# The last stage's normalisation beside the attention before it, and two jobs for GpSimd

## The chip, the cores and the metric

One core of a Trainium2 chip runs the whole program in one launch. The metric is the device time of one execution in microseconds (us). The engines are TensorE (PE, matmuls and transposes), VectorE (DVE), ScalarE (ACT), GpSimd (POOL) and SyncE (SP, which only issues transfers). Each engine works through its own list of instructions in order and waits on semaphores; a wait holds back everything behind it on that engine.

## The reference, cut to what matters

x is 128 sequences of 64 rows of 128 numbers. Four layers follow each other, each with an attention to a context and a feed-forward part, and each part adds `tanh(gate) * part(layernorm(x))` to x. The parts that the change touches:

```python
# layer 1, attention: 16 heads of 8 numbers; keys and values from the context z
x = x + tanh(g_xattn[1]) * softmax(q k^T / sqrt(8)) v Wfc        # q from layernorm(layernorm(x)), k, v from z
# layer 3, attention: one head, causal, the context as keys and values
scores = where(causal, q k^T, 0) / sqrt(128)
x = x + tanh(g_xattn[3]) * softmax(scores) v
# layer 3, feed-forward: 16-bit quantised activations, a scale over the WHOLE tensor
x = x + tanh(g_ffn[3]) * ffn(act_qdq(layernorm(x)))
def act_qdq(x):
    scale = max(max(abs(x)) / 32767, 1e-12)
    return clip(round(x / scale), -32768, 32767) * scale
```

The maximum in `act_qdq` is taken over all rows, so no quantised value of the last part can be made before the normalised rows of all sequences exist.

## The kernel before

The rows of two sequences make a tile of 128 rows; there are 64 tiles, all of x stays in the core's memory (`k.x`), and most stages work on groups of 4 tiles (16 groups, G = 16, 512 columns). The eight stages run one after the other: `attention0`, `experts0`, `attention1`, `spiking1`, `context_attention(2)`, `experts2`, `context_attention(3)`, `quantised3`. On each engine a stage begins with `stage_start`, a wait until the stage before has updated every tile (`x_updated`). Within a stage the order of the work is written out by hand: `steps(engine, n, lead, lag, body)` (and `unrolled`, which is the same) calls `body` for s = -lead .. n+lag-1, and `at(k)` in a body is the tile or group s+k if there is one. So each engine treats several groups at different points of their way in one step. Some names that the change touches:

- A normalisation has three parts. DVE takes statistics (`bn_stats`, L687 or L1143) and combines them (`bn_aggr`, L692 or L1149). GpSimd makes var + eps (L711 or L189) and its power -1/2 (L714 or L192), which is `rstd`. Then the normalised rows are made: in the attentions by DVE, (x - mean) * rstd, in `tile_xhat` (L198); in `quantised3` by ACT (L2099) from a factor and a shift that DVE writes (L2019, L2020).
- `attention1`, one tile for each step. DVE makes `KM` (L1168), the keys copied for 4 heads with the numbers of other heads set to zero, 128x512, for tile s+2. Its list in a step is: maxima of the first half of the scores of tile s (L1130), statistics of tile s+3 (L1143), subtraction (L1135), maxima and subtraction of the second half with L1149 between them, reciprocal (L1155, waits for PE's L1114), update of x (L1158), the scaled heads (L1163), KM (L1168), normalised rows of tile s+3 (L198). GpSimd makes only `rstd` of tile s+3. PE needs KM of tile s+2 two steps later.
- `context_attention(3)` (`masked`; layer 2 is `biased` and has the same code), one group for each step, s = -5 .. 16 on DVE: statistics of group s+5 (L687, L692), update of x for group s-1 (L1482, L1489, after PE's L1471), softmax of group s+2 (L1498 mask, L1502 maximum, L1506 subtraction), then the normalised rows of group s+5 (L198, four instructions), which wait for GpSimd's power. PE in a step: scores (L1436), queries (L1443), values (L1448), transposed rows of group s+4 (L1456), transposed weights (L1463), output (L1471). PE's scores of one group wait for the mask operation of the group before. In layer 2 GpSimd also adds a bias to x, 128x512 (L1417).
- `quantised3` begins with `normalise` over all groups: statistics on DVE, `rstd` on GpSimd, factor and shift on DVE, normalised rows of a group into `xhs` on ACT (L2099, four instructions), maximum of a group on DVE (L2010). After the last maximum, `scale_vector` and `scale_tensor` spread the overall scale over the partitions (first instruction L1896), and the two matmuls of the feed-forward part (L1955) begin.

Of the kernel before, what the change touches and what calls it, by code (L numbers as in the profile page):

```python
# [201 lines left out]
def stage_start(eng, k, no):  # L202

    if no:
        eng.wait_ge(*k.front(no)["x_updated"].all(0))
    if no == 1:
        eng.wait_ge(k.rest_loaded, k.rest_count)
        k.z1T_stored.wait_all(eng, k.T)

def prepare(k):
# [12 lines left out]

    k.w2_raw, k.w3_raw = keep(3 * D), keep(3 * D)
# [10 lines left out]
    k.q_raw = keep(3 * FF3).rearrange("p (w b i) -> p w b i", w=3, i=BLOCK)  # L237
    k.q_deq = keep(3 * FF3).rearrange("p (w b i) -> p w b i", w=3, i=BLOCK)
# [163 lines left out]
def attention0(k, no):  # L402
# [27 lines left out]
    def sync(sp):  # L430
# [16 lines left out]
        steps(sp, T, 3, 1, body)  # L447

    def gpsimd(pool):
# [12 lines left out]
        steps(pool, T, 2, 0, body)  # L462

    def tensor(pe):
# [70 lines left out]
        steps(pe, T, 2, 1, body)  # L535

    def vector(dve):
# [66 lines left out]
        steps(dve, T, 2, 1, body)  # L604

    def scalar(act):
# [35 lines left out]
        steps(act, T, 2, 1, body)  # L642
# [5 lines left out]
def sub(g, j):  # L648

    return Tile(g.idx * GROUP + j, j % 2)  # L650
# [86 lines left out]
class Combine:  # L737

    def __init__(self, k, f, experts, extra=False):

        self.k, self.f, self.experts, self.extra = k, f, experts, extra
        some = lambda slots, n: [k.take(n) for _ in range(slots)]
        self.scaled, self.pairs = some(2, 4 * D), some(2, 2 * D)
        self.rest, self.half = some(GROUP, D), some(2, D)
        self.s = k.sigs(k.T, dict(y_psum=1, scaled=4, summed=3 if extra else 2, acc=4))

    def scalar(self, act, g, j, coef, bank):  # L750
        s, t = self.s, sub(g, j)
        act.wait_ge(*s["y_psum"](t))
        if t.has(2):
            act.wait_ge(*s["summed"](t.back(2), 1))
        for i, e in enumerate(self.experts[1]):
            act.activation(self.scaled[t.par][:, i * D:(i + 1) * D], self.k.psum[:, bank, i * D:(i + 1) * D],
                           ACT.Copy, scale=coef[:, j, e:e + 1]).then_inc(s["scaled"].sem, 1)

    def gpsimd(self, pool, g, j, extra=None):
        s, t = self.s, sub(g, j)  # L760
        sc, pair, rest = self.scaled[t.par], self.pairs[t.par], self.rest[j]
# [1492 lines left out]
```

## Time and profile before

| | |
|---|---|
| time, median of 3 runs | 2120.57 us (2119.83 to 2121.06) |
| the profiled execution's own time | 2123.0 us |
| its span, first to last instruction | 2121.2 us |
| busy share of the span | PE 89%, DVE 79%, ACT 61%, POOL 12% |
| mean granted clock of TensorE | 0.946 of full speed |

A row of the timeline gives start, duration, engine, line, operation, output<-inputs, shapes and a count; successive instructions of one kind are merged (x4), and the duration is then from the start of the first to the end of the last. An instruction may start a little before the one ahead of it on its engine has ended, so work in an engine's step is best counted from start to start. Where an idle time stood ahead of an instruction, it is in brackets with what ended it.

### The profile page before, as it was taken

What the parts mean: (1) busy time and instruction counts of PE and PEld (TensorE: products, weight loads), DVE (VectorE), ACT (ScalarE), POOL (GpSimd) and SP (SyncE); (2) the same over time, 40 slices, a digit from 0 to 9 for tenths busy, and PEclk for the clock granted to TensorE, in tenths of its full rate; (3) what the DMA queues carried; (4) which work ended last, traced back from release to release, by engine and by line L of the source; (5) the groups of instructions that cost most, each with busy time, mean ns of one, the idle gap of its engine ahead of it and who ended that gap; (6) DMA issues with size and microseconds to landing.
All of it is one profiled execution on the core that took longest, in us unless ns stands there. A gap on an engine that the chain in (4) does not pass through costs nothing.

```text
span 2121.2 us, 47279 instructions
## 1 busy us (share of the span) xinstructions
PE 1897.6 (89%) x17713; PEld 1447.9 (68%) x17713; DVE 1669.4 (79%) x4756; ACT 1295.0 (61%) x3167; POOL 257.2 (12%) x551
## 2 busy tenths in 40 slices
PE   7999999999969989999989796999999993799608
PEld 5787887787759987878767574677677772344208
DVE  6787787787859969999957796777876498787894
ACT  5777777787752328888856464554455266108744
POOL 1111111111101111111111142000000023000000
PEclk9999999999979989999989898999999997899859
DMA  5222221111126631111100012322322120002452
GB/s 154 54 67 61 52 58 43 45 46 45 42 77 242 237 108 32 32 32 32 30 1 2 15 56 77 98 82 91 106 92 82 51 60 12 0 0 116 182 178 80
DMA packets 123395, 152.32 MB, mean 72 GB/s; under 512 B 45817, under 2 KB 98594, under 8 KB 121122
## 3 DMA queue, kind: packets, MB, share of 16 engines
q1 hardware_dynamic: 119986, 147.71, 22.5%
q8 instruction: 144, 2.36, 0.5%
q10 hardware_dynamic: 3184, 1.58, 0.3%
q14 instruction: 81, 0.66, 0.1%
HBM read 110.19 MB, written 22.28 MB: 62 GB/s over the span
## 4 chain that ended last, share of the span: by engine, by line
PE 68%; DVE 14%; DMA 6%; ACT 5%; issue 3%; POOL 2%; SPq 2%; POOLq 0%; ACTq 0%; DVEq 0%
PE banks L1638 7%; PE banks L1648 7%; PE banks L488 5%; PE banks L1955 4%; PE banks L527 4%; PE banks L477 3%; PE banks L1054 3%; PE banks L1114 3%; PE banks L1280 3%; PE banks L861 3%; PE banks L533 3%; PE banks L1289 3%; PE banks L500 2%; DMA arena<-arena 2%; PE banks L508 2%
## 5 line engine op out<-in xcount | busy, mean ns | idle before, releaser
L1813 ACT ACTIVATE arena<-banks,b1c 128x512 f32<-128x512 f32 x192 | 131.5, 687 | 141.7 <-PE banks L1638 140.1
L1742 DVE TENSOR_TENSOR arena<-arena 128x512 f32<-128x512 f32 (+1 forms) x256 | 170.4, 687 | 55.5 <-ACT arena L1813 48.4
L612 ACT ACTIVATE arena<-banks,arena 128x128 f32<-128x128 f32 x512 | 180.7, 373 | 1.2 <-DVE arena L559 1.2
L1648 PEld LDWEIGHTS banks<-w2a,arena 128*128 128x128 f32 x1024 | 122.0, 192 | 20.1 <-issue 20.1
L488 PE MATMUL banks<-arena,wk 128*128 128x128 f32 x1024 | 134.1, 285 | 1.5 <-DVE arena L583 1.5
L527 PE MATMUL banks<-wv,arena 128*128 128x512 f32 x256 | 131.0, 594 | 0.0
L488 PEld LDWEIGHTS banks<-arena,wk 128*128 128x128 f32 x1024 | 121.8, 195 | 12.7 <-issue 10.8
L861 PE MATMUL banks<-we,arena 128*128 128x128 f32 x1024 | 127.6, 283 | 0.8 <-DVE arena L931 0.2
L1648 PE MATMUL banks<-w2a,arena 128*128 128x128 f32 x1024 | 124.7, 275 | 0.0
L861 PEld LDWEIGHTS banks<-we,arena 128*128 128x128 f32 x1024 | 121.1, 196 | 4.0 <-DVE arena L931 3.3
L1638 PE MATMUL banks<-arena,w1s 128*128 128x512 f32 x256 | 122.9, 614 | 0.0
L533 PEld LDWEIGHTS banks<-konst,arena 128*128 128x128 f32 x512 | 58.9, 141 | 90.9 <-DVE arena L543 56.6
L559 DVE TENSOR_REDUCE arena<-banks 128x4 f32<-128x512 f32 x128 | 82.5, 686 | 36.3 <-PE banks L477 36.3
L612 ACT ACTIVATION_READ_ACCUMULATOR arena<-banks,arena 128x1 f32 x512 | 109.6, 214 | 0.0
L620 ACT ACTIVATE arena<-banks 128x512 f32<-128x512 f32 x64 | 38.2, 597 | 104.0 <-PE banks L488 104.0
L198 DVE TENSOR_SCALAR xhat<-x_tiles,mean_var,rstd 128x128 f32<-128x128 f32 x256 | 79.2, 341 | 27.8 <-POOL rstd L714 22.6
L714 POOL TENSOR_TENSOR rstd<-var_eps,konst 128x4 f32<-128x4 f32 x96 | 98.0, 1021 | 14.6 <-POOL var_eps L711 0.6
L1912 PE MATMUL banks<-konst,local_max 128*1 128x128 f32 (+1 forms) x4 | 1.4, 347 | 109.2 <-DVE local_max L1896 109.2
L711 POOL TENSOR_SCALAR var_eps<-mean_var 128x4 f32<-128x4 f32 x96 | 19.0, 198 | 653.1 <-DVE mean_var L692 651.0
L1955 PE MATMUL banks<-arena,wup 128*128 128x512 f32 x192 | 92.2, 618 | 0.7 <-ACT arena L2108 0.7
L543 DVE TENSOR_TENSOR arena<-arena 128x512 f32<-128x512 f32 x128 | 88.6, 692 | 4.4
L533 PE MATMUL banks<-konst,arena 128*128 128x128 f32 x512 | 80.2, 279 | 11.6 <-DVE arena L543 11.3
(253 smaller groups left out, 4980.1 us busy)
## 6 DMA issues: line engine op xcount, KB each, us to landing
arena<-coef_scratch SPq DMA_DIRECT2D x32, 2048.0 KB, 8.2
arena<-arena SPq DMA_DIRECT2D x256, 64.0 KB, 2.0
gated_scratch<-arena SPq DMA_DIRECT2D x16, 768.0 KB, 3.2
arena<-gated_scratch SPq DMA_DIRECT2D x16, 768.0 KB, 4.2
arena<-z1T_scratch SPq DMA_DIRECT2D x128, 64.0 KB, 2.3
arena<-in_ctx_turned SPq DMA_DIRECT2D x32, 256.0 KB, 2.9
arena<-in_ctx SPq DMA_DIRECT2D x64, 64.0 KB, 2.1
z1T_scratch<-arena SPq DMA_DIRECT2D x64, 64.0 KB, 1.6
```

The source lines that it names most:

```text
L488: mm = pe.matmul(ps[:, n, c * P:(c + 1) * P], k.wk0[:, c * P:(c + 1) * P], Z[t.idx % 3][:, :, n], start=True, stop=True)
L527: pe.matmul(ps[:, V0 + b, :], Z[t.idx % 3][:, b].rearrange("p s i -> p (s i)"), k.wv0[:, :], start=True, stop=True).then_inc(s["v_psum"].s ...
L533: mm = pe.transpose(ps[:, b, c * P:(c + 1) * P], prob[:, b, c * P:(c + 1) * P], k.ident)
L543: dve.tensor_tensor(each, each, rec[:, o].unsqueeze(2).broadcast_to([P, HPAIRS, P]), ALU.mult)\
L612: act.activation(prob[:, o, c * P:(c + 1) * P], ps[:, SCORES + o, c * P:(c + 1) * P], ACT.Exp, bias=low[:, o, c:c + 1], accum_out=total[:, ...
L714: pool.tensor_tensor(k.rstd[:, :, 0], k.ve[:, :, 0], k.konst[:, C_MHALF:C_MHALF + GROUP], ALU.pow).then_inc(f["rstd_ready"].sem, GROUP)
L861: mm = pe.matmul(ps[:, OUT + g.par, j * D:(j + 1) * D], xs[g.par][:, n, j * P:(j + 1) * P], k.we0[:, n, :], start=n == 0, stop=n == EXPERT ...
L1638: pe.matmul(ps[:, HID + c % NHID, :], w, xTg[g.par], start=True, stop=True).then_inc(s["h_psum"].sem, 1)
L1648: mm = pe.matmul(ps[:, OUT + g.par, j * D:(j + 1) * D], hT[g.par][:, c, j * P:(j + 1) * P], w, start=c == 0, stop=c == CHUNKS2 - 1)
L1742: dve.tensor_tensor(by_tile, by_tile, wide_coef[g.par][rows, e], ALU.mult).then_inc(s["scaled"].sem, 1)
L1813: act.activation(hT[g.par][:, c, :], ps[:, HID + c % NHID, :], ACT.Gelu, bias=k.b1c[:, c:c + 1])\
L1955: pe.matmul(ps[:, 1 + CHUNKS3 * n + c, :], w[:, c, :], xdT[:, g.idx, :], start=True, stop=True)\
```

## The change

1. `steps` becomes a generator that yields after each step how many are left. The stages of an engine are run in order as before, but for the last stage an engine may begin early: in the last steps of `context_attention(3)` it does one step of `quantised3`'s first part (`normalise`) after each of its own steps, on DVE for the last 16 steps, on GpSimd for the last 15, on ACT for the last 13. These three no longer wait for all of `context_attention(3)`; DVE's statistics wait for the x_updated of their own tile. PE and SP are not moved.
2. In `quantised3` the statistics use slot 1 of the shared small buffers and signals of their own, and GpSimd's list has a `normalise` of one group a step. Two weight buffers change places in the arena, so that `xhs` can be written early.
3. In `context_attention(3)` the normalised rows are made by GpSimd (four TENSOR_SCALAR of 128x128) right behind its power; mean and variance are kept in two buffers. Layer 2 keeps DVE for this.
4. In `attention1` KM is made by GpSimd, behind `rstd` in its step, and no longer by DVE.

```diff
 def steps(eng, n, lead, lag, body):
     for s in range(-lead, n + lag):
         body(lambda k: Tile(s + k, (s + k) % 2) if 0 <= s + k < n else None)
+        yield n + lag - 1 - s
...
+EARLY = {(7, "vector"): 16, (7, "gpsimd"): 15, (7, "scalar"): 13}
+def stage_start(eng, k, no, early):
+    if no > early:
+        eng.wait_ge(*k.front(no - early)["x_updated"].all(0))
...
@@ flamingo, run
+            for no, program in enumerate(programs):
+                beside = EARLY.get((no + 1, name), 0)
+                for left in program:
+                    if left < beside:
+                        next(programs[no + 1])
@@ attention1, gpsimd
             if t := at(3):
                 tile_rstd(k, f, pool, t, t.par, True)
+            if t := at(2):
+                wide = [P, PAIR, QUARTER, SEQ]
+                pool.wait_ge(*s["k_sb"](t))
+                if t.has(2):
+                    pool.wait_ge(*s["s_psum"](t.back(2)))
+                pool.tensor_tensor(KM[t.par], kT[t.par].rearrange("p (b i) -> p b i", b=PAIR).unsqueeze(2).broadcast_to(wide),
+                                   k.konst[:, C_MASK4:C_MASK4 + QUARTER].unsqueeze(1).unsqueeze(3).broadcast_to(wide),
+                                   ALU.mult).then_inc(s["km"].sem, 1)
@@ attention1, vector
-            if t := at(2):
-                wide = [P, PAIR, QUARTER, SEQ]
-                dve.wait_ge(*s["k_sb"](t))
-                dve.tensor_tensor(KM[t.par], kT[t.par]...,
-                                  ALU.mult).then_inc(s["km"].sem, 1)
             if t := at(3):
+                if t.has(2):
+                    dve.wait_ge(*f["xT_psum"](t.back(2)))
                 tile_xhat(k, f, dve, t, t.par)
@@ context_attention, gpsimd
-                if g := at(LEAD):
+                if masked and (g := at(LEAD)):
+                    last = sub(g, GROUP - 1)
+                    pool.wait_ge(*f["aggr"](last))
+                    pool.tensor_scalar(k.ve[:, :, 0], mv[g.par][:, :, 1], 1.0, EPS, ALU.mult, ALU.add)\
+                        .then_inc(f["vareps"].sem, GROUP)
+                    pool.wait_ge(*f["vareps"](last))
+                    if g.has(1):
+                        pool.wait_ge(*f["xhat_ready"](sub(g.back(1), GROUP - 1)))
+                    pool.tensor_tensor(k.rstd[:, :, 0], k.ve[:, :, 0], k.konst[:, C_MHALF:C_MHALF + GROUP],
+                                       ALU.pow).then_inc(f["rstd_ready"].sem, GROUP)
+                    pool.wait_ge(*f["rstd_ready"](last))
+                    if g.has(2):
+                        pool.wait_ge(*f["xT_psum"](g.back(2)))
+                    for j in range(GROUP):
+                        pool.tensor_scalar(xh[g.par][:, j * D:(j + 1) * D], k.x[:, sub(g, j).idx, :],
+                                           mv[g.par][:, j, 0:1], k.rstd[:, j, 0:1], ALU.subtract, ALU.mult)\
+                            .then_inc(f["xhat_ready"].sem, 1)
+                if biased and (g := at(LEAD)):
                     p_front(pool, g)
@@ context_attention, vector
+                    if masked and new.has(1):
+                        dve.wait_ge(*f["aggr"](sub(new.back(1), GROUP - 1)))
                     for j in range(GROUP):
                         d_front.stats(dve, new, j)
-                    d_front.aggr(dve, new)
+                    if masked:
+                        dve.wait_ge(*f["stats"](sub(new, GROUP - 1)))
+                        if new.has(2):
+                            dve.wait_ge(*f["xhat_ready"](sub(new.back(2), GROUP - 1)))
+                        for j in range(GROUP):
+                            dve.bn_aggr(mv[new.par][:, j, :], k.st[:, j, 0, :]).then_inc(f["aggr"].sem, 1)
+                    else:
+                        d_front.aggr(dve, new)
...
-                if new:
+                if new and biased:
                     if new.has(2):
                         dve.wait_ge(*f["xT_psum"](new.back(2)))
                     for j in range(GROUP):
                         tile_xhat(k, f, dve, sub(new, j), j, out=xh[new.par][:, j * D:(j + 1) * D])
@@ quantised3, gpsimd
+            g = at(0)
+            pool.wait_ge(*s["q_aggr"](g))
+            if g.has(1):
+                pool.wait_ge(*s["shift"](g.back(1)))
+            pool.tensor_scalar(k.ve[:, :, 1], k.mv[:, :, 1, 1], 1.0, EPS, ALU.mult, ALU.add)\
+                .then_inc(s["q_vareps"].sem, 1)
+            pool.wait_ge(*s["q_vareps"](g))
+            pool.tensor_tensor(k.rstd[:, :, 1], k.ve[:, :, 1], k.konst[:, C_MHALF:C_MHALF + GROUP], ALU.pow)\
+                .then_inc(s["q_rstd"].sem, 1)
@@ quantised3, vector (steps -2 .. 16)
+            if g := at(1):
+                dve.wait_ge(*s["q_rstd"](g))
+                if g.has(2):
+                    dve.wait_ge(*s["xhs"](g.back(2)))
+                dve.tensor_copy(affine[:, g.par, 0, :], k.rstd[:, :, 1]).then_inc(s["shift"].sem, 1)
+                dve.scalar_tensor_tensor(out=affine[:, g.par, 1, :], in0=k.mv[:, :, 1, 0], scalar=-1.0, in1=k.rstd[:, :, 1],
+                                         op0=ALU.mult, op1=ALU.mult).then_inc(s["shift"].sem, 1)
+            if b := at(-1):
                 dve.wait_ge(*s["xhs"](b))
                 dve.tensor_reduce(xmax[:, b.idx:b.idx + 1], xhs[:, b.idx, :], AX.X, ALU.max,
                                   apply_absolute_value=True).then_inc(s["xmax"].sem, 1)
+            if new := at(2):
                 for j in range(GROUP):
+                    dve.wait_ge(*f_before["x_updated"](sub(new, j)))
+                    dve.bn_stats(k.st[:, j, 1, :], k.x[:, sub(new, j).idx, :]).then_inc(s["q_stats"].sem, 1)
+                dve.wait_ge(*s["q_stats"](new))
+                for j in range(GROUP):
+                    dve.bn_aggr(k.mv[:, j, 1, :], k.st[:, j, 1, :]).then_inc(s["q_aggr"].sem, 1)
@@ quantised3, scalar
-            if g := at(1):
+            if g := at(0):
                 act.wait_ge(*s["shift"](g))
...
-        steps(act, G, 1, 0, normalise)
+        yield from steps(act, G, 0, 0, normalise)
```

## Rows read from the trace of the kernel before

**Rows 1.** Busy time of each engine in four stretches: attention1; three of context_attention(3) and after.

```profile
785.00:1066.00 281.00, 275.85 (x4287) 221.57 (x4286) 263.58 (x686) 243.09 (x633) 44.80 (x122) 0.98 0.14 31
1709.28:1756.12 46.84, 45.40 (x420) 36.74 (x419) 45.81 (x212) 29.53 (x61) 12.07 (x20) 1.00 0.20 58
1756.12:1771.80 15.68, 12.50 (x119) 11.03 (x117) 11.61 (x46) 8.81 (x17) 0.00 (x0) 1.00 0.06 18
1771.80:1810.87 39.07, 0.00 (x0) 0.00 (x0) 31.93 (x177) 26.36 (x64) 19.30 (x32) 0.53 0.00 1
```

**Rows 2.** Timeline of quantised3's normalisation, one of its groups, and its end.

```profile
1788.20 0.17 DVE L2019 COPY affine_of_norm<-rstd 128x4 f32<-128x4 f32 x1 [0.23 <-POOL rstd L714]
...
1788.47 0.38 DVE L692 BATCH_NORM_AGGREGATE mean_var<-bn_parts 128x2 f32<-128x6 f32 x4
1788.47 1.65 ACT L2099 ACTIVATE arena<-x_tiles,affine_of_norm 128x128 f32<-128x128 f32 x4 [0.70 <-DVE affine_of_norm L2020]
1788.76 0.65 DVE L2010 TENSOR_REDUCE xmax<-arena 128x1 f32<-128x512 f32 x1
...
1790.42 0.17 DVE L2019 COPY affine_of_norm<-rstd 128x4 f32<-128x4 f32 x1 [0.23 <-POOL rstd L714]
...
1810.87 0.17 DVE L1896 TENSOR_REDUCE local_max<-xmax 128x1 f32<-128x16 f32 x1
```

**Rows 3.** Timeline of context_attention(3), DVE in one steady step.

```profile
1718.65 0.87 DVE L687 BATCH_NORM_STATS2 bn_parts<-x_tiles 128x6 f32<-128x128 f32 x4
...
1719.85 0.21 DVE L1482 RECIPROCAL arena<-banks 128x2 f32<-128x2 f32 x2
...
1721.07 0.41 DVE L1498 TENSOR_TENSOR arena<-banks,konst 128x256 f32<-128x256 f32 x1
...
1721.97 0.42 DVE L1506 TENSOR_TENSOR arena<-arena 128x256 f32<-128x256 f32 x1
...
1722.31 1.11 DVE L198 TENSOR_SCALAR arena<-x_tiles,mean_var,rstd 128x128 f32<-128x128 f32 x4
```

**Rows 4.** Timeline of the same stage, PE's first output and DVE's first update.

```profile
1706.48 1.06 PE L1471 MATMUL banks<-arena 128*128 128x129 f32 x8
...
1710.48 0.20 DVE L1482 RECIPROCAL arena<-banks 128x2 f32<-128x2 f32 x2
```

**Rows 5.** Groups of GpSimd's instructions, whole span.

```profile
L714 POOL TENSOR_TENSOR rstd<-var_eps,konst 128x4 f32<-128x4 f32 x96 | 98.0, 1021 | 14.6 <-POOL var_eps L711 0.6
...
L1417 POOL TENSOR_TENSOR arena<-x_tiles,bout 128x512 f32<-128x512 f32 x16 | 20.3, 1270 | 7.4 <-DVE x_tiles L1489 7.4
L711 POOL TENSOR_SCALAR var_eps<-mean_var 128x4 f32<-128x4 f32 x96 | 19.0, 198 | 653.1 <-DVE mean_var L692 651.0 <-ACT xhat L980 2.1
...
L1407 POOL MEMSET arena<- 128x512 f32 x4 | 2.0, 528 | 100.6 <-DVE x_tiles L1785 74.7 <-DVE x_tiles L1310 25.9
```

**Rows 6.** Timeline of context_attention(2), DVE's work beside GpSimd's L1417.

```profile
1236.14 1.27 POOL L1417 TENSOR_TENSOR arena<-x_tiles,bout 128x512 f32<-128x512 f32 x1
1236.29 0.42 DVE L1506 TENSOR_TENSOR arena<-banks,arena 128x256 f32<-128x256 f32 x1
1236.63 1.63 DVE L198 TENSOR_SCALAR arena<-x_tiles,mean_var,rstd 128x128 f32<-128x128 f32 x4
```

**Rows 7.** Timeline of attention1, one step of DVE, and GpSimd's power in it.

```profile
907.18 0.17 DVE L1149 BATCH_NORM_AGGREGATE mean_var<-bn_parts 128x2 f32<-128x6 f32 x1
...
907.72 0.54 POOL L192 TENSOR_TENSOR rstd<-var_eps,konst 128x1 f32<-128x1 f32 x1
...
908.50 0.68 DVE L1168 TENSOR_TENSOR arena<-arena,konst 128x512 f32<-128x512 f32 x1
909.10 0.34 DVE L198 TENSOR_SCALAR xhat<-x_tiles,mean_var,rstd 128x128 f32<-128x128 f32 x1
...
911.35 0.18 DVE L1149 BATCH_NORM_AGGREGATE mean_var<-bn_parts 128x2 f32<-128x6 f32 x1
```

**Rows 8.** Waits in attention1: engine, line and what it waited for, us in total, times, longest.

```profile
DVE arena L1155 <- PE banks L1114: 12.8, 35, 1.3
```

More of the change, by code:

```diff
@@ L208, in stage_start, with stage_program @@
         k.z1T_stored.wait_all(eng, k.T)
+def stage_program(eng, k, no, name, part):
+    stage_start(eng, k, no, (no, name) in EARLY)
+    yield from part[name](eng)
 def prepare(k):
@@ L797, in unrolled @@
-def unrolled(n, lead, lag, body):
-    for s in range(-lead, n + lag):
-        body(lambda k: Tile(s + k, (s + k) % 2) if 0 <= s + k < n else None)
 def experts0(k, no):
@@ L851, in body @@
                 p_front(pool, g)
-        unrolled(G, 4, 0, body)
+        yield from steps(pool, G, 4, 0, body)
     def tensor(pe):
@@ L956, in body @@
                 weigh(nxt, 3, EXPERTS)
-        unrolled(G, 4, 1, body)
+        yield from steps(dve, G, 4, 1, body)
     def scalar(act):
@@ L1121, in body @@
                 weights_turned(t, 0)
-        steps(pe, T, 2, 2, body)
+        yield from steps(pe, T, 2, 2, body)
     def vector(dve):
@@ L1264, in body @@
                 p_front(pool, g)
-        steps(pool, G, 3, 0, body)
+        yield from steps(pool, G, 3, 0, body)
     folds = Folds(k)
@@ L1328, in body @@
                 update(g)
-        steps(dve, G, 3, 1, body)
+        yield from steps(dve, G, 3, 1, body)
     def scalar(act):
@@ L1347, in body @@
                     act.activation(sq[g.par][:, c, :], relu[:, c, :], ACT.Square).then_inc(s["sq"].sem, 1)
[L1348 removed]
+        yield from steps(act, G, 2, 0, body)
     return dict(gpsimd=gpsimd, tensor=tensor, vector=vector, scalar=scalar)
[L1354 to L1357 removed]
 def context_attention(layer):
@@ L1381, in stage @@
         mx, rec = two(GROUP), k.take(GROUP)
+        mv = [v.rearrange("p (j n) -> p j n", j=GROUP) for v in two(2 * GROUP)] if masked else None
         A, B = k.A[layer - 2], k.B[layer - 2]
@@ L1626, in body @@
                 p_front(pool, g)
-        steps(pool, G, 3, 0, body)
+        yield from steps(pool, G, 3, 0, body)
     def tensor(pe):
@@ L1976, in first @@
                 project(pe, g, s["p_psum"], freed, (1,))
-        steps(pe, G, 1, 0, first)
+        yield from steps(pe, G, 1, 0, first)
         scale_tensor(pe, "ug")
@@ L1984, in tensor @@
         pe.wait_ge(*s["pmax"].all(G))
-        steps(pe, G, 0, 0, second)
+        yield from steps(pe, G, 0, 0, second)
         scale_tensor(pe, "gs")
@@ L2039, in first @@
                 dve.tensor_scalar(xd[:, :], xq[:, :], scale["x"][:, :], None, ALU.mult).then_inc(s["xd"].sem, 1)
-        steps(dve, G, 2, 0, first)
+        yield from steps(dve, G, 2, 0, first)
         dve.wait_ge(*s["pmax"].all(G))
@@ L2055, in second @@
                     .then_inc(s["gsmax"].sem, 1)
-        steps(dve, G, 0, 0, second)
+        yield from steps(dve, G, 0, 0, second)
         dve.wait_ge(*s["gsmax"].all(G))
@@ L2108, in first @@
                 act.activation(xdT[:, g.idx, :], ps[:, 0, :], ACT.Copy).then_inc(s["xdT"].sem, 1)
-        steps(act, G, 1, 0, first)
+        yield from steps(act, G, 1, 0, first)
         scale_known(act, "ug")
@@ L2125, in second @@
                 act.activation(sig[g.par], gq[g.par], ACT.Sigmoid, scale=scale["ug"][:, 1:2]).then_inc(s["sig"].sem, 1)
-        steps(act, G, 0, 0, second)
+        yield from steps(act, G, 0, 0, second)
         scale_known(act, "gs")
```

156 lines of the change are left out of this document (41 added, 115 removed).

## The prediction

> **What bounds the kernel now.** I read four views, in this order. The busy times by stretch show who is full where [rows 1]. In attention1 PE (275.85 of 281 us) and DVE (263.58) are both nearly full. In the steady part of context_attention(3) they are again (45.40 and 45.81 of 46.84). Then come 39.07 us, from the last update of x to the first instruction of the overall scale, in which PE does nothing, DVE is busy 31.93, ACT 26.36 and GpSimd 19.30. Nothing can hide those 39 us, since the scale needs the maximum of all groups. The timeline of that stretch shows the loop: one group takes about 2.2 us, from one L2019 to the next [rows 2], and half of that is the way through GpSimd and back. The timelines of the two attentions give DVE's step from start to start: 3.66 us before the normalised rows and 1.03 for them, 46.84 / 10 = 4.68 in all [rows 1, 3]; and 911.35 - 907.18 = 4.17 us in attention1 [rows 7]. The groups of GpSimd and its timeline beside DVE give the prices of what is moved there [rows 5, 6].
>
> **The stretch of 39.07 us.** It shrinks to what must follow the last update. DVE's last early step does affine 0.27 (L2019 to L692 in [rows 2]), a maximum 0.57 (0.65, but a DVE instruction starts 0.08 before the end of the one ahead, as L198 behind L1506 [rows 3]), statistics and their combination 1.20 (1719.85 - 1718.65 [rows 3]): 2.04. Then the way through GpSimd, from L692 to the next L2019 without the 0.38 of L692: 1790.42 - 1788.47 - 0.38 = 1.57; affine 0.27; ACT's rows 1.65; the last maximum 0.65 [rows 2]. Sum 6.2. **Term: -32.9.**
>
> **The steps of context_attention(3).** DVE loses L198, 1.03 a group, and GpSimd gets it. DVE gains in its steps 4 to 15 the same 2.04 us; in step 1 only the 1.20 of statistics, in steps 2 and 3 1.47.
> - Steps 1 to 10, before 46.84: 3.66 + 1.20 = 4.86, twice 3.66 + 1.47 = 5.13, seven times 3.66 + 2.04 = 5.70. Sum 55.0. **Term: +8.2.**
> - Step 11 to the last update, before 15.68 [rows 1]. Steps 11 to 13 have an update and a softmax, 1722.31 - 1719.85 = 2.46 [rows 3], and 2.04: 4.50 each. Steps 14 and 15 have an update, 1721.07 - 1719.85 = 1.22, and 2.04: 3.26 each. The last update 1.22. Sum 21.2. PE's waits in this part are then hidden. **Term: +5.6.**
> - Start of the stage. Before, PE starts its first output at 1706.48, but DVE comes to the first update only at 1710.48 [rows 4], because each of its first steps waits for GpSimd's power and then makes the rows itself. Now DVE makes 1.20 of statistics and 1.24 of softmax in such a step and is there first; half of the output is there 0.5 us after its start, and PE itself may be a little earlier. I take 4.0 (3 to 5). **Term: -4.0.**
>
> What must keep up beside DVE's 5.70: PE needs under 4.68 (it fits into that now). ACT has 29.53 / 10 = 2.95 by its busy time and 3.2 with all of a step counted, and 1.65 more: under 4.9. GpSimd has two powers with their additions, 2 x 1.4 (0.20 and 1.02 with handovers [rows 5]), and four TENSOR_SCALAR of 128x128, whose duration no row shows. By the slope of MEMSET, (528 / 512) ns an element on top of 198 ns, one takes 0.33 us; by that of the two-input L1417, 1270 / 512, 0.52 [rows 5]. I take 0.4, near the first, as it reads one tensor: 2.8 + 1.6 = 4.4; at the upper bound 4.9. So GpSimd, too, keeps up, up to 0.72 us for one. The order of waits is sound: GpSimd's power for a group of the last stage is asked for at the end of a DVE step and wanted 3.66 us later, against 1.57 for the way; behind that wait on GpSimd stand the rows for PE, which are wanted a step later.
>
> **A shared door.** While L1417 reads on GpSimd, DVE's four L198 take 1.63 us instead of 1.11: the first stood until L1417 was over. In the same time L1506, with one input in PSUM, took its usual 0.42 [rows 3, 6]. In context_attention(3) L1506 has both inputs in SBUF (arena<-arena [rows 3]), and it would come, 3.3 us into the step, into the middle of GpSimd's four instructions (2.7 to 4.3). No row shows this meeting. Bounds: 0, as in [rows 6] for L1506; and 1.0, the rest of the burst, for 10 steps. I take 0.3, a part of one instruction. **Term: +3.0 (0 to 10).**
>
> A rule of the Trainium skill speaks against the change here ("SBUF — State Buffer", section "Who interferes with whom"): a DVE instruction with two SBUF inputs contends with a GpSimd instruction that reads SBUF, and the second to issue blocks entirely. By the rule L1506 and the small L2020 would wait for one of GpSimd's 0.4 us each, some +4 to +7 for the stage; by the row of L1506 alone nothing. The trace has a block of this kind for L198 only.
>
> **KM on GpSimd.** DVE loses L1168: 0.60 from start to start. But the door is in the way. GpSimd's power ends at 907.72 + 0.54 = 908.26 and KM, whose keys are long there, starts at once; at the 1270 ns of L1417, also 512 columns of two inputs [rows 5], it ends at 909.53. DVE comes to its L198 at 908.50, where KM stood [rows 7]. In [rows 6] an L198 that came 1.27 - 0.49 = 0.78 before the end of L1417 cost 0.52 more, so the delay is the remaining time less 0.26: here 1.03 - 0.26 = 0.77. DVE's step is 4.17 - 0.60 + 0.77 = 4.34: longer than before. For 62 tiles that is +10.5, where DVE is what binds. In 35 of the steps it stood for PE before the reciprocal, 12.8 us in all [rows 8]; there L198 comes later, and the 0.17 vanishes: -6. Where DVE is slower, PE gets ahead and waits less: -2. **Term: +2.5 (0 to 8; -6 if nothing blocked, because PE, full for 275.85 of 281 us [rows 1], leaves no more).** Each 0.1 us more of KM costs 6 us from here on.
>
> **Sum.** -32.9 + 8.2 + 5.6 - 4.0 + 3.0 + 2.5 = -17.6. The profiled execution (span 2121.2, own time 2123.0) would come to 2105.4. It is 2.4 us above the median of the runs, 2120.57, so for the median: 2103.0. TensorE's clock I leave out: it is 0.53 of full in the empty stretch and 1.00 in the two before, of which one has PE busy for only 12.50 of 15.68 us, 80%, as much as it would be in the longer steps (under 4.68 of 5.70). The pause before the scale stays, if shorter, and the first matmuls start slow as before. The swap of two buffers and the generator cost nothing: no instruction is added.
>
> **Rivals.**
> 1. *Nothing blocks* (8%). DVE and GpSimd pass each other in the new pairs. Then the +3.0 goes and attention1 gains up to 6: -17.6 - 3.0 - 8.5 = -29, 2091.5. Against it: [rows 6], the very instruction that is left behind KM.
> 2. *The longer steps stretch* (15%). GpSimd's rows take 0.9 us each or the door costs the whole rest of the burst: 2.8 + 3.6 = 6.4 against 5.70 is +7 for ten steps, the burst likewise up to 10 instead of 3. Result -17.6 + 7 = -10.6, 2110. For it: GpSimd's power takes 1.02 us for 4 columns [rows 5], so its cost doesn't follow columns. Against: MEMSET and L1417 do follow them.
> 3. *KM paces attention1: slower than before* (11%). KM has two broadcast inputs and more dimensions than L1417. DVE's step is 3.07 + KM; the gain of 17.6 is used up when KM takes 0.29 us more than 1.27. From 1.56 us on the kernel is not faster; at 1.8 us it is +33 - 17.6 = +15, 2136. For it: GpSimd's price for this form is in no row. Against: the same operation, types and 512 columns at 1270 ns in the mean of 16.
> 4. *The early part isn't early* (3%). If a wait ties the last stage's steps to the end of the stage before, the 39 us return and only the start (-4) and L198 remain: within 0.2%. The waits in the change name only things one or two groups old, so I see no such tie.
>
> **How the numbers follow.** Forecast 63%: 2103.0, by the bounds of its terms 2098 to 2110. The range takes in rival 2 and the way to rival 1 but for its last 1.5 us, and leaves out most of 3 and 4: 2093 to 2115. A measurement of this kernel can tell about 0.2%, 4.2 us. Faster: forecast, rivals 1 and 2, 0.86. Same: 0.04. Slower: rival 3 beyond its point and little else, 0.10.
>
> **What the profile after would show.** From the last update to L1896's counterpart about 6 us instead of 39. DVE's step in context_attention(3) near 5.7 to 6.0 and full; the first update about 0.5 us behind the start of PE's first output instead of 4.0. GpSimd's TENSOR_SCALAR at 0.33 to 0.52 us; over 0.72, rival 2. In attention1 KM at 1.27 us, and L198 near 1.1 us instead of 0.34 in most steps; at 0.34 throughout, rival 1. The stretch of attention1 283 to 284 us instead of 281; over 300, rival 3. The forecast fails if KM's price or the block is off by a few tenths, since 62 tiles multiply it, or if the early steps wait for ACT's rows or GpSimd's power instead of running full.

## The result, and the profile after

The changed kernel takes 2108.26 us (median of 5 runs, 2106.05 to 2112.19); the kernel before, on the same chip, 2120.37 (5 runs). The ratio is 0.9939, interval 0.9924 to 0.9954: 13 us faster, where 17.6 were forecast. Run again beside the experiments it was at 0.9921 (0.9906 to 0.9937). The profiled execution has a span of 2105.4 us against 2121.2.

Busy times of the kernel after, in five stretches: attention1 from the first L1102 to the last (L1149 before), context_attention(3) from its first statistics to the first update of x, the ten steps to update 10, from there to the end of the last update, and from there to the first instruction of the overall scale. Columns: start and end, length, busy PE, PEld, DVE, ACT, POOL with counts, granted clock, DMA share, GB/s.

```profile
775.40:1043.20 267.80, 260.58 (x4086) 212.23 (x4087) 242.62 (x608) 232.65 (x608) 109.77 (x197) 0.98 0.15 33
1679.50:1706.70 27.20, 18.54 (x131) 12.51 (x133) 12.91 (x69) 12.85 (x23) 24.92 (x38) 0.81 0.17 49
1706.70:1766.40 59.70, 46.91 (x439) 37.78 (x436) 52.30 (x269) 42.75 (x93) 54.84 (x79) 1.00 0.16 46
1766.40:1789.20 22.80, 14.66 (x119) 12.38 (x117) 20.52 (x98) 18.08 (x43) 9.57 (x16) 0.85 0.04 13
1789.20:1795.50 6.30, 0.00 (x0) 0.00 (x0) 4.12 (x17) 3.29 (x8) 1.34 (x3) 0.50 0.00 0
```

The same stretches of the kernel before, from the same instructions: 275.6, 24.86, 45.67, 15.48 and 39.07 (first statistics at 1685.79, first update at 1710.65, just behind the L1482 of [rows 4]). So the idle 39 us have become 6.30, but the ten steps grew by 14.0 and the part behind them by 7.3. In those ten steps GpSimd (54.84 of 59.70) is the fullest engine, ahead of DVE (52.30). These are rows of one step of them, in the timeline of the kernel after: GpSimd's, DVE's around its wait, and the waits of PE and ACT. The window ends ahead of GpSimd's fourth row instruction.

```profile
1744.68 0.66 PE L1417 MATMUL banks<-konst,arena 128*128 128x128 f32 x4 [1.52 <-POOL arena L1370]
1744.71 0.20 POOL L1916 TENSOR_SCALAR var_eps<-mean_var 128x4 f32<-128x4 f32 x1
1744.99 1.03 POOL L1919 TENSOR_TENSOR rstd<-var_eps,konst 128x4 f32<-128x4 f32 x1
...
1745.24 0.42 DVE L1467 TENSOR_TENSOR arena<-arena 128x256 f32<-128x256 f32 x1
...
1745.37 0.60 ACT L1520 ACTIVATE arena<-banks 128x512 f32<-128x512 f32 x1 [1.48 <-PE banks L1417]
...
1746.05 0.17 DVE L1983 COPY affine_of_norm<-rstd 128x4 f32<-128x4 f32 x1 [0.39 <-POOL rstd L1919]
...
1746.11 0.20 POOL L1359 TENSOR_SCALAR var_eps<-arena 128x4 f32<-128x4 f32 x1
...
1746.44 1.01 POOL L1364 TENSOR_TENSOR rstd<-var_eps,konst 128x4 f32<-128x4 f32 x1
...
1747.56 2.35 POOL L1370 TENSOR_SCALAR arena<-x_tiles,arena,rstd 128x128 f32<-128x128 f32 x3
```

GpSimd pauses in it for nothing but handovers, 0.08 to 0.14 us ahead of an instruction: addition and power for the last stage (L1916, L1919), addition and power for this stage (L1359, L1364), then the rows (L1370, counterpart of L198). The others wait for it: DVE's L1983 (L2019 before) for the last stage's power, PE's L1417 (L1456 before) for the rows. L1916 comes again at 1750.77, so the period is 6.06 us. What L1370 and KM cost, from the view of one line (shortest, median, longest ns; first and last start):

```profile
L1370 POOL TENSOR_SCALAR arena<-x_tiles,arena,rstd x64: 787/792/1050, 1682.5 to 1768.1; 128x128 f32<-128x128 f32 x64
L998 POOL TENSOR_TENSOR arena<-arena,konst x64: 1038/1040/1042, 779.7 to 1047.8; 128x512 f32<-128x512 f32 x64
```

0.79 us for a row instruction where I had taken 0.4, and 1.04 for KM where I had taken 1.27. The first costs at the start of the stage too, where GpSimd's timeline after shows no other pause either:

```profile
1699.93 0.19 POOL L1359 TENSOR_SCALAR var_eps<-arena 128x4 f32<-128x4 f32 x1
1700.26 1.03 POOL L1364 TENSOR_TENSOR rstd<-var_eps,konst 128x4 f32<-128x4 f32 x1
1701.40 3.12 POOL L1370 TENSOR_SCALAR arena<-x_tiles,arena,rstd 128x128 f32<-128x128 f32 x4
1704.60 0.19 POOL L1359 TENSOR_SCALAR var_eps<-arena 128x4 f32<-128x4 f32 x1
```

A group every 4.67 us. The first update, forecast 4.0 us earlier, comes 2.3 later. In attention1 a step of DVE, with KM on GpSimd (counterpart of [rows 7]):

```profile
906.36 0.17 DVE L1102 BATCH_NORM_AGGREGATE mean_var<-bn_parts 128x2 f32<-128x6 f32 x1
...
907.40 1.04 POOL L998 TENSOR_TENSOR arena<-arena,konst 128x512 f32<-128x512 f32 x1
...
907.81 0.71 DVE L199 TENSOR_SCALAR xhat<-x_tiles,mean_var,rstd 128x128 f32<-128x128 f32 x1
...
910.53 0.17 DVE L1102 BATCH_NORM_AGGREGATE mean_var<-bn_parts 128x2 f32<-128x6 f32 x1
...
911.50 0.26 DVE L1108 RECIPROCAL arena<-banks 128x16 f32<-128x16 f32 x1 [0.17 <-PE banks L1067]
```

L199 (L198 before) takes 0.71 instead of 0.34: the block is there, and L199 ends 0.08 behind KM. But KM is over 2.08 us behind L1102 (908.44 - 906.36), where 2.35 was forecast (909.53 - 907.18), and L199 comes 0.13 later in the step than forecast, so the block costs 0.37 and not 0.77. The stretch is 7.8 us shorter, not 2.5 longer; the experiments show that only about half of the 7.8 is KM's.

### The profile page after: what moved, and what is told of

The parts are those of the page before. It is cut to its first block and busy times, and to the rows that moved or that the text cites. A ratio compares the mean times of both kernels' runs of the same rounds, so it can differ in the third digit from the quotient of the medians.

```text
span 2105.4 us, 47401 instructions
## 1 busy us (share of the span) xinstructions
PE 1896.9 (90%) x17713; PEld 1449.0 (69%) x17713; DVE 1637.6 (78%) x4628; ACT 1292.3 (61%) x3167; POOL 371.8 (18%) x679
## 3 DMA queue, kind: packets, MB, share of 16 engines
HBM read 110.19 MB, written 22.28 MB: 63 GB/s over the span
## 5 line engine op out<-in xcount | busy, mean ns | idle before, releaser
L199 DVE TENSOR_SCALAR xhat<-x_tiles,mean_var,rstd 128x128 f32<-128x128 f32 x256 | 97.1, 411 | 30.9 <-POOL rstd L725 20.9
L722 POOL TENSOR_SCALAR var_eps<-mean_var 128x4 f32<-128x4 f32 x64 | 12.6, 197 | 572.1 <-DVE mean_var L703 570.0
L467 POOL TENSOR_SCALAR var_eps<-mean_var 128x1 f32<-128x1 f32 x64 | 12.2, 190 | 502.3 <-DVE mean_var L566 502.3
L1083 DVE TENSOR_REDUCE arena<-banks 128x8 f32<-128x512 f32 x128 | 87.8, 686 | 8.5 <-PE banks L1020 6.5
L594 DVE TENSOR_SCALAR arena<-banks,affine_columns 128x128 f32<-128x128 f32 x192 | 67.0, 404 | 29.3 <-PE banks L528 27.6
```

The lines of the kernel that those rows point to most:

```text
L199: dve.tensor_scalar(k.xh[:, slot, :] if out is None else out, k.x[:, t.idx, :], k.mv[:, slot, 0, 0:1], k.rstd[:, slot, 0:1], ALU.subtract, ...
L1083: dve.tensor_reduce(mx[:, n].rearrange("p (r h) -> p r h", r=2), scores(n), AX.X, ALU.max)\
```

## Experiments

My theory at this point: (a) GpSimd's row instruction at 0.79 us makes GpSimd the pace of context_attention(3), and the way of the rows through it isn't worth its price; (b) KM gains because DVE's step falls below PE's, so that the block costs nothing that binds. The rivals are, for (a), that DVE or the shared door sets the 6.06 us, and for (b), that the block is what is left to gain.

**km_only and overlay_only: the two halves.** km_only is the kernel before with only KM moved. overlay_only is the change with KM and the rows of context_attention(3) back on DVE.

```diff
 # overlay_only, in context_attention (and KM back in DVE's list of attention1)
-                if masked and (g := at(LEAD)):     # GpSimd: power and rows
+                if False and (g := at(LEAD)):
-                if biased and (g := at(LEAD)):     # GpSimd: power alone
+                if g := at(LEAD):
...
-                if new and biased:                 # DVE: rows
+                if new:
```

> The kernel before with one part of the change: KM of attention1 made by GpSimd, all else as before. In the changed kernel attention1's statistics run from 775.4 to 1043.3 us instead of 775.1 to 1050.7. If that is due to KM alone, this kernel is 7 to 8 us faster than before, about 2113, and DVE's normalised rows take 0.6 to 0.7 us in most steps, since they wait for the end of GpSimd's KM. If the term of the prediction stood (+2.5), it would be about 2123.

> The change without its two moves to GpSimd: the last stage's normalisation runs beside context_attention(3), but DVE makes that attention's normalised rows and KM itself. Theory (GpSimd's four instructions of 0.79 us pace the changed kernel, 6.06 us a step): here DVE paces, 5.70 + 1.03 = 6.73 us in steps 4 to 10, the first update comes 24.9 us after the first statistics as before instead of 27.1, and the stage and the normalisation together take about as long as in the changed kernel, 115 to 117 us; the whole is 8 to 9 us faster than before, about 2112. Rival (the overlap needs the rows on GpSimd): DVE's steps get longer than the sum, and at most 4 us are gained.

km_only: 2119.45 us, ratio 0.9985 (0.9972 to 0.9998), so 0.4 to 6 us faster, not the 7 to 8 that I expected. Its attention1 is 269.5 long (one wait of 3.9 us for a transfer in it), 6.1 less than before; the median distance from one tile's combination of statistics (L1149) to the next falls from 4.365 to 4.231. The medians hide a pattern: most steps alternate, between 4.17 and 4.37 us in the kernel before, and between 4.17 and 4.23 with KM on GpSimd, with longer, irregular steps among them. overlay_only: 2112.45 us, ratio 0.9949 (0.9932 to 0.9967). Its busy times from first statistics to the scale:

```profile
1686.15:1710.99 24.84, 20.57 (x158) 14.81 (x159) 18.46 (x91) 13.96 (x27) 8.35 (x17) 0.86 0.18 53
1710.99:1773.77 62.78, 46.06 (x424) 37.06 (x421) 61.45 (x308) 41.17 (x91) 22.91 (x38) 1.00 0.15 43
1773.77:1794.93 21.16, 11.64 (x102) 9.51 (x102) 20.39 (x99) 17.46 (x41) 7.07 (x12) 0.94 0.04 13
1794.93:1801.23 6.30, 0.00 (x0) 0.00 (x0) 4.10 (x17) 3.29 (x8) 1.37 (x3) 0.50 0.00 0
```

Now DVE is full (61.45 of 62.78), with steps of 6.59, and the whole is 115.08 against 115.94 with the rows on GpSimd. So the overlay makes all of the gain there, and moving the rows none: 3.1 us less in the ten steps, 2.3 more ahead of them, 1.6 more behind. The halves, 0.15% and 0.51%, add up to 0.66%; the change gave 0.61 and 0.79.

overlay_only also says what KM is worth. Its attention1 has KM on DVE and steps of 4.17 and 4.37, as before, and is yet only 271.7 us long instead of 275.6. With KM on GpSimd the stretch is 266.9 to 269.8 long in all eleven kernels that were traced. So of the 7.8 us of the change some 2 to 5 are KM's (3.9 against overlay_only), which is also what km_only's time says. The rest came without KM's move, and lies in the irregular steps: what the irregular steps take above 4.37 us adds up to 8.8 us in the trace before, 5.3 in overlay_only and 4.1 in the change.

**km_after_rows and km_doubled: what the block costs.** In the one GpSimd makes KM only after DVE's rows of the step, so that they never meet; in the other it makes KM twice, the first time into a spare buffer.

```diff
 # km_after_rows
+                if at(3):
+                    pool.wait_ge(*f["xhat_ready"](at(3)))
                 pool.tensor_tensor(KM[t.par], ...)
 # km_doubled
+                pool.tensor_tensor(spare[t.par], ...)      # the same operands
                 pool.tensor_tensor(KM[t.par], ...)
```

> The changed kernel, but GpSimd starts KM of a tile only when DVE has made the normalised rows of the next one, so that the two never meet. Theory (KM's reading holds DVE up): DVE's rows take 0.34 us in every step instead of 0.63 to 0.71, DVE's list gets 0.3 us shorter, and attention1 goes to PE's own 4.16 us a tile from 4.25: 1 to 5 us faster than the changed kernel. Rival (the longer rows have another cause): they stay at 0.6 or more and the time does not move. If KM comes too late for PE, scores wait and it is slower.

> The changed kernel, with the product of KM made twice by GpSimd, first into a spare buffer, then into its place; output the same. GpSimd then has some 2.9 us of work in a step of 4.25. If DVE's rows wait until GpSimd has no more reading to do, a step of DVE grows by 1.0 us, and the kernel is 50 to 65 us slower than the changed one. If they wait only for the instruction that runs when they come, nothing or up to 0.1 us a step is added (0 to 6 us). If there is no such wait at all, nothing is added.

km_after_rows: ratio 0.9948 (0.9931 to 0.9966), not faster than the change, where 1 to 5 us were expected. The views of its L199, its L1104 and its waits in attention1 (us in total, times, longest):

```profile
L199 DVE TENSOR_SCALAR xhat<-x_tiles,mean_var,rstd x64: 335/336/347, 783.5 to 1050.8; 128x128 f32<-128x128 f32 x64
L1104 DVE BATCH_NORM_AGGREGATE mean_var<-bn_parts x64: 168/172/182, 780.9 to 1049.3; 128x2 f32<-128x6 f32 x64
...
DVE arena L1085 <- PE banks L1022: 24.5, 61, 1.6
```

The block is gone from every step (0.336), and the stretch is 268.4 long, as in the change. The 0.3 us that DVE saves a step it stands before PE's scores (24.5 us in 61 waits). In two such steps, 4.17 and 4.24 us long, PE is busy throughout and DVE for 3.69 in each. PE is the pace, and theory (b) holds. km_doubled: 2111.62 us, ratio 0.9947 (0.9926 to 0.9968), attention1 269.8. Its timeline:

```profile
910.09 1.04 POOL L999 TENSOR_TENSOR arena<-arena,konst 128x512 f32<-128x512 f32 x1
910.51 0.70 DVE L199 TENSOR_SCALAR xhat<-x_tiles,mean_var,rstd 128x128 f32<-128x128 f32 x1
911.09 1.04 POOL L1002 TENSOR_TENSOR arena<-arena,konst 128x512 f32<-128x512 f32 x1
```

L199 waits for the instruction that runs, and is let in ahead of the next: two KMs in a row block no longer than one. So a burst of these costs DVE at most the rest of one instruction. That speaks against the price behind my upper bound for context_attention(3), the whole rest of the burst; beside the row instructions themselves the block is shorter still (last section).

**first_rows_dve, one_power and both: taking work off GpSimd.** In the first, DVE makes the rows of the first six groups, as before, since it stands idle there; in the second, one power of 128x8 serves a group of this stage and the last stage's group seven behind it, and GpSimd's own list of the last stage skips its first nine groups.

```diff
 # first_rows_dve (FIRST = 6)
-                    for j in range(GROUP):
+                    for j in range(GROUP if g.idx >= FIRST else 0):     # GpSimd
-                if new and biased:
+                if new and (biased or new.idx < FIRST):                 # DVE
 # one_power
+                    both = g.idx >= 7
+                    if both:
+                        b, q = g.back(7), k.last_stage
+                        ...      # q_aggr of b, its addition, shift of b's forerunner
-                    pool.tensor_tensor(k.rstd[:, :, 0], k.ve[:, :, 0], ..., ALU.pow)
+                    pool.tensor_tensor(k.rstd[:, :, :], k.ve[:, :, :], ..., ALU.pow)    # if both
```

> The changed kernel, but in context_attention(3) DVE makes the normalised rows of the first six groups, as it did before, and GpSimd only those from group 6 on. Theory (GpSimd's 4 x 0.79 us and its power, 4.67 us a group, hold the start up): the first update comes 24.9 us after the first statistics instead of 27.2, and the kernel is 2 to 4 us faster than the changed one. Rival (PE's own start sets it): no change in that distance.

> The changed kernel, with one power of 4x2 columns on GpSimd for both stages in the steps in which it works for both, instead of two of 4. Theory (GpSimd paces the steps at 6.06 us: two times some 1.45 for the powers with their additions and 3.15 for the rows): a power of 8 columns costs some 1.6 us by 0.54, 0.70 and 1.02 for 1, 2 and 4 columns, GpSimd's step falls to about 5.5, and DVE, at 5.56 by the kernel with the overlap only (6.59 less 1.03), takes over: 5.6 us a step, 4 us less in all. Rival (DVE or the way of the waits paces): steps stay at 6.0.

> The normalised rows of the first six groups of context_attention(3) on DVE, as in first_rows_dve, and one power of 128x8 for both normalisations of a step, as in one_power. If both gains have the cause that I name (GpSimd full in its loop at the start of the stage, and full again with two powers in each later step) and do not overlap, they add: first update 24.8 us after the first statistics, not 27; updates 0 to 10 in 55 instead of 57 to 60, with later steps of 5.66 us in which DVE is full; first statistics to the scale 107, against 116 for the change, 111 for each alone; time 8 to 9 us below the change, a ratio to the kernel before of 0.987 to 0.989. Rival: the steps are paced by something that neither edit touches, and the two together give no more than the better of them, 0.9898.

| | time, us | ratio (interval) | to update 0 | to 10 | to the last | first statistics to scale |
|---|---|---|---|---|---|---|
| the change again | 2108.06 | 0.9921 (0.9906 to 0.9937) | 26.92 | 59.73 | 22.80 | 115.74 |
| first_rows_dve | 2102.97 | 0.9898 (0.9881 to 0.9916) | 24.76 | 56.96 | 22.82 | 110.83 |
| one_power | 2105.24 | 0.9914 (0.9895 to 0.9933) | 26.90 | 56.90 | 21.44 | 111.54 |
| both | 2096.87 | 0.9871 (0.9846 to 0.9895) | 24.75 | 54.52 | 21.43 | 107.00 |

By the stretches each edit shortens the part that it touches and the two add (4.9 and 4.2 us alone, 8.7 together), so GpSimd was the pace. In the time one_power alone can't be told from the change. One power of 8 columns costs 1.66 us where two of 4 cost 2.04; with the handovers the step falls from 6.06 to 5.66. Both together are the first kernel that beats the change clearly. In its timeline a step of GpSimd is

```profile
1745.59 0.20 POOL L1360 TENSOR_SCALAR var_eps<-arena 128x4 f32<-128x4 f32 x1
1745.87 0.20 POOL L1366 TENSOR_SCALAR var_eps<-mean_var 128x4 f32<-128x4 f32 x1
1746.20 1.66 POOL L1375 TENSOR_TENSOR rstd<-var_eps,konst 128x8 f32<-128x8 f32 x1
1747.97 3.17 POOL L1385 TENSOR_SCALAR arena<-x_tiles,arena,rstd 128x128 f32<-128x128 f32 x4
1751.25 0.19 POOL L1360 TENSOR_SCALAR var_eps<-arena 128x4 f32<-128x4 f32 x1
```

still without a pause, 5.66 from start to start.

**forms_on_gpsimd: the price of each form.** The change, with GpSimd doing forms of its own, each twice, behind all its work. In order of their lines, L2179 to L2192: TENSOR_SCALAR with two constants (multiply, add), one constant, one pointer, two pointers (subtract, multiply: the form of the rows); the last with 256 and with 64 columns; TENSOR_TENSOR with 128 and 256 columns; three of 256 with broadcast inputs, whose rows are not shown; and a power of 8 columns.

```diff
+            probe(lambda: pool.tensor_scalar(out, src, 1.5, 0.5, ALU.mult, ALU.add))
+            probe(lambda: pool.tensor_scalar(out, src, 1.5, None, ALU.mult))
+            probe(lambda: pool.tensor_scalar(out, src, col, None, ALU.mult))
+            probe(lambda: pool.tensor_scalar(out, src, col, col2, ALU.subtract, ALU.mult))
...
```

> The changed kernel with twelve forms of GpSimd instructions, each twice and each waited for, added behind GpSimd's own work, in a stretch in which it has nothing to do; the output is the same. It asks why a TENSOR_SCALAR of 128x128 takes 0.79 us where the slope of MEMSET gave 0.33 and that of the two-input L1417 0.52. If the price is in the two scalars that come from memory, the form with two constants takes 0.3 to 0.5 us; if it is in the second operation, the form with one operation does; if each element costs it, 64 columns take half. Broadcast inputs: if they are why KM takes 1.04 us and L1417 1.27, the forms of 256 columns with broadcast are 0.1 us shorter than that without.

The groups of its instructions by form (count, busy us and mean ns of one, then idle time):

```profile
L2192 POOL TENSOR_TENSOR var_eps<-var_eps,konst 128x8 f32<-128x8 f32 x2 | 3.3, 1653 | 0.2
...
L2183 POOL TENSOR_SCALAR spare<-konst,gates 128x256 f32<-128x256 f32 x2 | 3.0, 1512 | 0.2
...
L2182 POOL TENSOR_SCALAR spare<-konst,gates 128x128 f32<-128x128 f32 x2 | 1.6, 820 | 0.2
...
L2186 POOL TENSOR_TENSOR spare<-konst 128x256 f32<-128x256 f32 x2 | 1.3, 634 | 0.2
...
L2181 POOL TENSOR_SCALAR spare<-konst,gates 128x128 f32<-128x128 f32 x2 | 1.2, 597 | 0.2
L2184 POOL TENSOR_SCALAR spare<-konst,gates 128x64 f32<-128x64 f32 x2 | 1.2, 580 | 0.2
L2180 POOL TENSOR_SCALAR spare<-konst 128x128 f32<-128x128 f32 x2 | 1.1, 535 | 0.2
L2185 POOL TENSOR_TENSOR spare<-konst 128x128 f32<-128x128 f32 x2 | 0.9, 452 | 0.2
...
L2179 POOL TENSOR_SCALAR spare<-konst 128x128 f32<-128x128 f32 x2 | 0.6, 302 | 0.1
```

With two constants the form costs 0.30, near my lower bound from MEMSET. With one pointer (L2181) it costs 0.60, with two (L2182) 0.82, more than a TENSOR_TENSOR of the same columns (L2185, 0.45); from 128 to 256 columns it grows by 5.4 ns a column, TENSOR_TENSOR by 1.4. The rows do not say why. With one multiplication a pointer in place of the constant adds only 0.06 (L2180, L2181), and one constant is dearer (0.54) than two (0.30); the step from one pointer to two also adds the subtraction. Broadcast inputs are no single answer either: at 256 columns two of the three broadcast forms took 0.61 and one 0.73, against 0.63 without. The Trainium skill ("GPSIMD Engine Reference", section "4.1 Engine selection") has one-input work on GpSimd at roughly line rate and two-input work at twice VectorE's time. By it a row instruction would be the cheaper form, and here it is the dearer, 0.82 against 0.45; for two inputs KM's 1.04 against DVE's 0.68 [rows 7] is a factor of 1.5.

**rows_in_two and all_three: the rows in the cheaper form.** A subtraction and a multiplication of 128x512, both TENSOR_TENSOR with a broadcast operand, instead of four row instructions; alone, and with the two edits above.

```diff
-                    for j in range(GROUP):
-                        pool.tensor_scalar(xh[...], k.x[...], mv[...][:, j, 0:1], k.rstd[:, j, 0:1], ALU.subtract, ALU.mult)
+                    pool.tensor_tensor(rows, k.x[4 tiles], mean.broadcast_to(wide), ALU.subtract)
+                    ...      # the wait for it
+                    pool.tensor_tensor(rows, rows, rstd.broadcast_to(wide), ALU.mult)
```

> The change, but GpSimd makes the rows of a group with two TENSOR_TENSOR of 128x512 (minus the mean, times rstd, both broadcast over the columns) in place of four TENSOR_SCALAR of 128x128 with two pointers. My theory: the row form's price (0.80 us each, 3.19 a group) is what makes GpSimd full. TENSOR_TENSOR took 0.45 us at 128 columns and 0.61 to 0.73 at 256 in the probes, and 1.04 (broadcast) to 1.27 at 512 in the kernel: 2.1 to 2.5 a group. GpSimd's step falls from 6.06 to 4.9 to 5.4, DVE's 5.66 binds, the first update comes at 24.9 after the first statistics or sooner; first statistics to the scale 109 to 111; time 5 to 6 us below the change, ratio 0.990 to 0.9915. Rival: GpSimd's two-input form shuts DVE's two-input subtraction out for a whole microsecond each; then DVE's step grows by up to 1 us and nothing is gained.

> first_rows_and_one_power with the rows of the later groups in two TENSOR_TENSOR as well. DVE is full in its steps with any one of the edits; so with the theory this gives nothing over first_rows_and_one_power (within 1 us; steps 5.66 us, first statistics to scale 106 to 108). Were GpSimd still what paces the steps there, it would be 3 to 5 us faster than that.

rows_in_two: 2096.86 us, ratio 0.9878 (0.9853 to 0.9902), better than expected: first update after 22.28, ten steps 56.40, 21.16, and 106.14 in all. all_three: 2101.96 us, ratio 0.9907 (0.9881 to 0.9933), where I expected nothing lost: 24.76, then 61.50 (steps of 6.50), and 113.71 in all. Its timeline says why:

```profile
1747.87 1.63 POOL L1375 TENSOR_TENSOR rstd<-var_eps,konst 128x8 f32<-128x8 f32 x1
1749.53 0.17 DVE L2014 COPY affine_of_norm<-rstd 128x4 f32<-128x4 f32 x1
1749.58 1.04 POOL L1386 TENSOR_TENSOR arena<-x_tiles,arena 128x512 f32<-128x512 f32 x1
1749.61 1.03 DVE L2015 SCALAR_TENSOR_TENSOR affine_of_norm<-mean_var,rstd 128x4 f32<-128x4 f32 x1
1750.56 0.67 DVE L2019 TENSOR_REDUCE xmax<-arena 128x1 f32<-128x512 f32 x1
```

One power releases both GpSimd's subtraction and DVE's factor and shift. GpSimd starts 0.03 ahead, and DVE's L2015, 128x4 and 0.15 us of work, stands for the whole instruction, in every step: with 5.56 us of its own work it comes to 5.56 + 0.88 = 6.44, against steps of 6.50. In rows_in_two the two engines drift against each other; steps 5 to 7 are 5.56, and where they meet (the timeline of step 9, below) steps 8 and 9 are 6.4 and 7.0.

```profile
1746.93 1.04 POOL L1370 TENSOR_TENSOR arena<-x_tiles,arena 128x512 f32<-128x512 f32 x1
1747.25 1.00 DVE L1470 TENSOR_TENSOR arena<-arena 128x256 f32<-128x256 f32 x1
1748.12 1.04 POOL L1374 TENSOR_TENSOR arena<-arena,rstd 128x512 f32<-128x512 f32 x1
1748.17 1.01 DVE L1986 COPY affine_of_norm<-rstd 128x4 f32<-128x4 f32 x1
```

So the rival that I gave rows_in_two, the shut door, is real; there it strikes in 3 of the ten steps (8 to 10), in all_three in nearly all. rows_in_two and first_rows_and_one_power (2096.86 and 2096.87) can't be told apart; both beat the change and the kernel before.

## Why the prediction was right, and where it wasn't

The side was right and the time inside the range, but not by its own steps: attention1 came out 10.3 us better than forecast, and the three terms of context_attention(3) together 10.8 worse. That they nearly cancel is luck. Forecast and measured in the profiled execution:

| term | forecast | measured |
|---|---|---|
| empty stretch | -32.9 (to 6.2) | -32.8 (to 6.30) |
| steps 1 to 10, with the door | +8.2 and +3.0 | +14.0 |
| to the last update | +5.6 | +7.3 |
| start of the stage | -4.0 | +2.3 |
| attention1 | +2.5 | -7.8 |
| elsewhere | 0 | +1.2 |
| sum, by the spans | -17.6 | -15.8 |

- **The stretch of 39.07 us.** Right, to 0.1 us, in all its parts: the way through GpSimd, ACT's rows and one maximum are what is left.
- **"So GpSimd, too, keeps up, up to 0.72 us for one"**: the step that failed. Its rule was right and the size wrong: at 0.79 the sum 2.8 + 3.2 = 6.0 is the 6.06 of the trace. I took 0.4 from MEMSET and from a two-input form, 0.33 to 0.52, and no end of that range held a form with two pointers. This is rival 2, to which I gave 15%; its +7 for ten steps was worked out at 0.9 us; at 0.79, 10 x (5.96 - 5.70) is 2.6. Measured, it is 5.8 (14.0 - 8.2), and most of it lies in the first steps, where GpSimd paces too: steps 2 to 4 take 6.44, 6.28 and 6.88 us (from update to update), where I had 5.13, 5.13 and 5.70 by DVE alone, 3.6 in all. Steps 5 to 9, at 6.06, give 1.8.
- **To the last update, +5.6.** The 1.7 on top are step 11: 6.04 us where I had 4.50. GpSimd is still behind there; with the rows in two (rows_in_two) this step takes 4.39.
- **DVE's steps.** 5.70 forecast; where GpSimd is out of the way (rows_in_two) it is 5.56, and in first_rows_and_one_power the ten steps are 54.52 - 45.67 = +8.9 longer than before, against +8.2.
- **The shared door, +3.0.** Too much in this kernel, where it is under 1 in the ten steps. In most of them L1467 comes beside GpSimd's power and takes its usual 0.42; beside a row instruction it takes 0.50 once, and its longest of all 16, ahead of the ten, is 0.64. A price near the upper bound appears only with another form, in all_three. The door also holds GpSimd up, which I had left out: in steps 3 and 4 its addition comes just behind L1467 and takes 0.42 and 0.43 instead of 0.20.

```profile
1719.95 0.42 DVE L1467 TENSOR_TENSOR arena<-arena 128x256 f32<-128x256 f32 x1
...
1720.01 0.42 POOL L1916 TENSOR_SCALAR var_eps<-mean_var 128x4 f32<-128x4 f32 x1
```

- **Start of the stage, -4.0.** The reason (DVE no longer waits and makes rows) was sound: DVE's reciprocal for the first update now starts 0.64 us behind PE's first output (1706.15 and 1705.51), not 4.0. But I forgot to ask what GpSimd's pitch is there: 1.47 for addition and power and 3.20 for rows, from start to start, 4.67 a group, longer than DVE's 3.9 before. first_rows_dve, which leaves the rows on DVE there, gets 2.2 back ahead of the first update and 2.8 in the steps behind it.
- **KM, +2.5.** The mis-sized term is KM's 1.27. My own formula, 3.07 + KM, gives at 1.04 a step of 4.11, below PE's 4.17 and 4.23. From there the block is free, as km_after_rows shows. The step before wasn't always 4.17: that was a short one, and every second step took 4.37, with a wait of 0.17 for PE in it. What KM's move takes away is the 0.14 between 4.37 and 4.23 in every second step, 31 x 0.14 = 4.3 us at most, near the 3.9 of overlay_only against the change. The other 3.9 of the measured -7.8 came to overlay_only too, with KM on DVE. The block's rule (remaining time less 0.26) was right: 908.44 - 907.81 + 0.34 - 0.26 = 0.71.
- **The rivals.** Nothing of 3 and 4 came: KM was cheaper, and the early steps ran. Rival 1's price for attention1 (-6) came near, but not its reason: the block was there and PE was the pace.
- **Not shown.** Why the profiled execution loses 1.2 us in the other stages; such differences come between runs of one kernel too. The clock was granted at 1.00 in the ten steps, as I had taken it, but at 0.85 behind them (1.00 in both before), where PE was busy for 14.66 of 22.80 us; PE isn't the pace there.

## What to carry to other kernels

An engine that has been nearly idle has prices that its old work doesn't show: before work is given to it, the exact form is to be measured (constants or pointers, one wide instruction or four), since here the form decides by a factor of 2.7. Work moved out of an idle stretch pays at once; work moved between engines pays only as far as the receiver stays under the new step, and at the start of a stage the receiver's pitch can be what everyone waits for. When two engines share a door, what matters is the moment: the short instruction that needs it should be released by another event than the long one, though no run here tried that by itself.

## What the runs showed of the hardware that I had not expected

- The door depends on the form at GpSimd. Beside a TENSOR_TENSOR of 128x512 these DVE instructions, all with inputs in SBUF, begin only 0.1 to 0.3 us before GpSimd ends: COPY and SCALAR_TENSOR_TENSOR of 128x4, TENSOR_SCALAR of 128x128, TENSOR_TENSOR of 128x256. DVE's statistics, TENSOR_REDUCE and the instructions that read PSUM pass. Beside GpSimd's power (1.01 us, 4 columns) L1467 took its usual 0.42 where it came 0.25 us behind the power's start. Beside the two-pointer row instruction the door is shut only at first: in the kernel after L1467 came 0.08, 0.22 and 0.24 us behind the start of one (at 1693.43, 1708.61 and 1768.31) and took 0.64, 0.50 and 0.48. With 0.42 of its own it was let in 0.29 to 0.30 us behind that start each time, some 0.5 before the end, and so it was in six other traces; where it came 0.39 us or more behind the start it took its 0.42. The Trainium skill ("SBUF — State Buffer", section "Who interferes with whom") says that the second to issue waits for the whole of the first; the trace agrees for the wide TENSOR_TENSOR and not for the other two.
- The door is given up between two instructions of GpSimd: a DVE instruction that waits goes ahead of GpSimd's next (km_doubled).
- GpSimd's power costs 0.54, 0.70, 1.02 and 1.66 us for 1, 2, 4 and 8 columns: 0.16 us a column on top of 0.38. So the one of 8 columns saves 0.38 against two of 4, no more.
